# Attention stage of a fused layer: one column-tiled group of value and denominator products late in each unit, in place of several

## The reference

```python
dots = jnp.einsum('bhid,bhjd->bhij', q, k) * d ** (-0.5)
dots = jnp.where(mask[None, None], mask_value, dots)
attn = jax.nn.softmax(dots, axis=-1)
out = jnp.einsum('bhij,bhjd->bhid', attn, v)
...
shared = jax.nn.silu(xf @ sh_gate_w) * (xf @ sh_up_w) @ sh_down_w
```

## Time and profile before

| | us |
|---|---|
| time, median of 3 runs | 5415.98 (5410.62 to 5418.36) |
| the profiled execution: its span | 5418.5 |
| time before stage B's first shared-expert matmuls | about 720 |
| stage B, to its last denominator matmul | about 720 to 2447 |
| PE busy in the span | 5303.0 (98%) |
| DVE busy | 3828.9 (71%) |
| ACT busy | 2615.1 (48%) |
| POOL busy | 3028.9 (56%) |

### The profile page before, as it was taken

How to read it: one execution, slowest core, us unless ns; L and a number is a source line. 1 busy time by engine, 2 the same in 40 slices (tenths; PEclk the granted TensorE clock), 3 DMA queues, 4 the chain that set the end, 5 groups by cost and what they waited for, 6 DMA issues and landing times. The chain is left out here.

```text
span 5418.5 us, 102292 instructions
## 1 busy us (share of the span) xinstructions
PE 5303.0 (98%) x32880; PEld 4440.9 (82%) x32880; DVE 3828.9 (71%) x7311; ACT 2615.1 (48%) x3833; POOL 3028.9 (56%) x2716
## 2 busy tenths in 40 slices
PE   8999989999999999998999999999999999999999
PEld 6888866766666667667999999989999999999786
DVE  6666667778787877775676666766667666666664
ACT  3333333333343333335666666666666666666410
POOL 1222215666666665115777777777777777777514
PEclk9999989999999999998999999999999999999999
DMA  7777764444454444435676677767787676676748
GB/s 239 248 242 255 250 173 129 133 134 119 136 148 135 119 141 118 134 98 119 134 158 112 134 170 150 163 132 167 158 227 158 135 164 129 134 156 113 178 154 289
DMA packets 500414, 864.75 MB, mean 160 GB/s; under 512 B 64388, under 2 KB 165493, under 8 KB 497694
## 3 DMA queue, kind: packets, MB, share of 16 engines
q1 hardware_dynamic: 356014, 567.12, 33.2%
q0 software_dynamic: 140928, 292.13, 29.5%
q10 hardware_dynamic: 3312, 3.47, 0.3%
HBM read 498.49 MB, written 330.47 MB: 153 GB/s over the span
## 5 line engine op out<-in xcount | busy, mean ns | idle before, releaser
L1754 POOL DMA_INDIRECT mid_base<-e_rows,e_ox x556 | 1160.3, 2087 | 372.5 <-POOL e_ox L1749 239.5
L1865 DVE TENSOR_TENSOR e_wgu_lo<-e_wgu,e_wgu_hi 128x2048 fp32r<-128x2048 f32 x278 | 637.5, 2293 | 806.4 <-ACT e_wgu_hi L1788 676.6
L1742 POOL DMA_INDIRECT e_xg<-mid_xn,e_ix x556 | 625.5, 1125 | 336.4 <-POOL e_ix L1739 226.4
L1801 ACT CAST e_xT_hi<-e_ps_t 128x512 fp32r<-128x512 f32 x556 | 299.1, 590 | 929.8 <-PE e_ps_t L1931 929.8
L1069 POOL DMA_INDIRECT mid_ids<-b_pairs,b_cell x512 | 614.3, 1200 | 141.8 <-issue 141.0
L1944 PE MATMUL e_ps_g<-e_xT_hi,e_wgu_hi 128*128 128x256 f32 x2224 | 652.9, 294 | 1.7 <-issue 1.7
L1944 PE MATMUL e_ps_g<-e_xT_lo,e_wgu_hi 128*128 128x256 f32 x2224 | 630.0, 283 | 0.0
L1944 PE MATMUL e_ps_g<-e_xT_hi,e_wgu_lo 128*128 128x256 f32 x2224 | 629.7, 283 | 0.0
L1944 PE MATMUL e_ps_u<-e_xT_hi,e_wgu_hi 128*128 128x256 f32 x2224 | 629.4, 283 | 0.0
L1944 PE MATMUL e_ps_u<-e_xT_lo,e_wgu_hi 128*128 128x256 f32 x2224 | 629.4, 283 | 0.0
L1944 PE MATMUL e_ps_u<-e_xT_hi,e_wgu_lo 128*128 128x256 f32 x2224 | 629.4, 283 | 0.0
(11 more groups left out here) (286 smaller groups left out, 13368.0 us busy)
## 6 DMA issues: line engine op xcount, KB each, us to landing
b_xT_hi<-mid_xT_hi SPq DMA_DIRECT2D x32, 1024.0 KB
b_xT_lo<-mid_xT_lo SPq DMA_DIRECT2D x32, 1024.0 KB
mid_base<-b_x SPq DMA_DIRECT2D x32, 1024.0 KB
e_wgu<-in_gate_w SPq DMA_DIRECT2D x62, 512.0 KB
e_wgu<-in_up_w SPq DMA_DIRECT2D x62, 512.0 KB
e_wd<-in_down_w SPq DMA_DIRECT2D x62, 512.0 KB
ec_cell<-mid_base SPq DMA_DIRECT2D x88, 256.0 KB, 4.9
ab_q<-mid_q_hi SPq DMA_DIRECT2D x82, 256.0 KB, 4.0
```

Of the source, the lines that this page charges most:

```text
L1742: pool.indirect_dma_start(xg[s][:, i, :], None, t["xn"], bass.IndirectOffsetOnAxis(ap=ix[s][:, i:i + 1], axis=0))\
L1754: pool.indirect_dma_start(t[f"base{i}"], bass.IndirectOffsetOnAxis(ap=ox[s][:, i:i + 1], axis=0), rows[s][:, i, :], None, compute_op=ALU.a ...
L1801: act.copy(xT_hi[s][:, i * DC // 2 * RB:(i + 1) * DC // 2 * RB], ps_t[i][:, :]).then_inc(xT_hi_ready, 1)
L1865: dve.tensor_tensor(wgu_lo[s][:, :], wgu[s][:, :], wgu_hi[s][:, :].bitcast(F32), ALU.subtract)\
```

## The change

A table says in which slot each unit's groups stand. Units n = 0, 1 and 2 have all their values and the denominators in one place, in slots 7, 9 and 11. Unit n = 3 has two places: slot 6 with the diagonal and block 0, and slot 12, that is slot 0 of the next unit, with blocks 1 and 2 and the denominators. An item has 5 places where it had 14. The work itself, the other matmuls, and the program order of DVE, ACT, POOL and SP are the same.

```diff
+        TILED = {0: {7: [0]}, 1: {9: [1, 0]}, 2: {11: [2, 0, 1]}, 3: {6: [3, 0], SLOTS: [1, 2]}}
+
         def pv_slots(n, k):
-            if k == 6:
-                return [n]
-            return [kt for kt in range(n) if 7 + 2 * kt == k]
+            return TILED[n].get(k, [])
...
+            def tiled(u, k):
+                n = u % NCH
+                for kt in pv_slots(n, k):
+                    values(u, kt)
+                if k == max(TILED[n]):
+                    denominators(u)
+
...
-                    for kt in pv_slots(n, k):
-                        values(u, kt)
-                    if k == 7 and n == 0:
-                        denominators(u)
-                    if k == 0 and u and (u - 1) % NCH:
-                        denominators(u - 1)
+                    if k == 0 and u:
+                        tiled(u - 1, SLOTS)
+                    tiled(u, k)
...
-            denominators(NU - 1)
+            tiled(NU - 1, SLOTS)
```

## The result

The changed kernel takes 5486.0 us (median of 4 runs, 5479.11 to 5494.25), the kernel before in the same comparison 5417.17 (5410.62 to 5419.56). The ratio is 1.0127, 95% interval 1.0115 to 1.0140: 1.3% slower, some 69 us. The profiled execution's span is 5488.8 us, its time 5490.64.

A forecast was written before the change was run, and what follows sets the result against it. Up to slot 8 of units n = 1 and 2 DVE sets the pace, afterwards PE. 5418.5 + 30 (exposed groups) + 32 (clock falls) = 5480.5 profiled, less 2.5 for the median: 5478 us, range 5430 to 5508.

The forecast's parts named there:

- the forecast case: Whole kernel: exposed groups add 30 us and clock falls 32 us, giving 5478 us; chance 0.49.
- Front set by DVE, tail by PE: Units n = 1 and 2: DVE sets the pace up to slot 8, hiding groups; PE sets it from there on.
- Price of a group: On PE: a lone group costs 1.19 us, a further joined one 0.88; 143 joins at 0.31 save 44 us.
- that rule alone: Rival, PE alone sets the pace: the change only removes drains, all 44 us count, 5372 us; chance 0.11.
- Unit by unit: PE time per unit: n = 0 +1.51, n = 1 +2.65, n = 2 +1.60, n = 3 -3.88; +1.88 us an item, +30 in all.
- The clock: Idle before slot 8, n = 1 and 2: 19 of 32 gaps halve PE's clock, 1.70 us each, 32 us.
- The Trainium skill's warning: Gaps before slot 8: it warns only of longer idle gaps; by it the clock stays, leaving the 30 us alone.
- Waits said to cost nothing: Denominators behind DVE's add, SP's loads and stores, POOL's multiplication and ACT's buffers: added or moved waits cost nothing beside the rest.

The follow-up runs named there:

- The experiment with the later add: Changed kernel with DVE's first add_past of units n = 1 and 2 moved from slot 6 to slot 8: 5382.07 us, ratio 0.9935.
- The run with n = 3 alone: Kernel before with only the units n = 3 as in the changed kernel, n = 0, 1 and 2 as before: 5400.24 us, ratio 0.9962.
- The run with the filler: Changed kernel with two matmuls of constants into ps_d at the end of slot 7 of units n = 1 and 2: 5448.48 us, ratio 1.0058.
- the run with the later reciprocals: Kernel with the first add moved to slot 8, plus two of DVE's four reciprocals of n = 0, 1, 2 moved to slots 9 and 10: 5579.95 us.
- with n = 1 alone: Kernel before with only the units n = 1 as in the changed kernel, n = 0, 2 and 3 as before: 5458.89 us, ratio 1.0077.

## Why the prediction was right

5478 us were forecast, 5486.0 measured, within the range and with the sign; the forecast case came, not a rival. By its steps:

- **Front set by DVE, tail by PE.** Right. PE idles before slot 8 as forecast at about 2.1 us: 2.05 in unit 25. The experiment with the later add shows that in the changed kernel it is the add's place, not DVE's load, that sets slot 8. One thing is missing in it: in the kernel before, PE with its groups was as late as DVE, so the front was not DVE's alone, and moving the add there gave nothing (5420.37).
- **Price of a group.** Right: 0.88 and 0.86 us for further groups in a set. The run with n = 3 alone gave -21 us for 48 joins (15 expected). The Trainium skill (TensorEngine Tiling (Array Packing), section Key Properties) says that a change of tiling mode drains the engine; that run agrees in kind. By that rule alone the whole change would have given 5372; it names a cost, not what hides it.
- **Unit by unit.** The run with the filler has no clock falls, so it shows the terms by themselves: n = 0 +1.61 (forecast +1.51), n = 1 +2.72 (+2.65), n = 2 +1.29 (+1.60), n = 3 -3.70 (-3.88), together +1.92 an item (+1.88). In time it is +32 us against +30.
- **The clock.** Right in kind, mis-sized in both factors: 25 falls, not 19, at 1.5 us each, not 1.70. The product is 37.5 instead of 32. The count came from 3 of 5 gaps of like length elsewhere, which is a small sample; the price took half of each stretch as lost, but the step goes from 0.23 to 0.43 us, less than double, which makes it 1.6. One factor was too low and the other too high, so that the product came this near is in part luck. Some 65 us at half clock were forecast, 25 stretches of 3.4 us make 85.
- **The Trainium skill's warning** (TensorE: Matmul & The Clock Gate, section Why this matters for your kernels) concerns gaps longer than these. The measurement decides: gaps of 1.77 to 2.32 us lowered the clock in 25 of 32 places, and filling them gave 37.5 us back.
- **Waits said to cost nothing.** Right for the denominators, for ACT and POOL, though slot 11's set starts 6.4 us behind slot 8's first matmul at full clock (1455.83 to 1462.23 in the run with the filler), not over 7; the add still ends before it, at 1460.51. SP's queue had slack in this change; in the run with the later reciprocals some 12 us more of delay were more than it had.

The size of the miss, 8 us, is the clock's 5.5 and the units' 2.

What stays open is which gaps lower the clock: in n = 1 a gap of 2.02 us left it at 1.00 and one of 1.92 didn't, and with n = 1 alone 7 of 16 counted instead of 11. Length alone doesn't settle it, and no run here was made to tell more.

## What to carry to other kernels

An engine that is 98% busy need not be the one that sets the pace: find for each stretch which wait ends last, and before moving work out of a stretch ask whether it was hidden there. Work that only fills another engine's delay is free where it stands and costs in full elsewhere, so shorten what it was filling (here, one add placed behind the work that PE waits for) together with moving it: here neither step alone made the kernel faster. Or leave it there, joined: that gained nearly as much. And follow an engine's results through the in-order DMA queue before delaying them: what stands behind a store there is delayed too.

## What the hardware showed that was not expected

- TensorE waits of 1.77 to 2.32 us, between dense matmuls, came in 25 of 32 places with 3.4 us at 1.2 GHz. Two useless full-width matmuls in each of them kept 2.4 GHz and made the kernel 37.5 us faster.
- A fall cost less than half of its stretch, 1.5 of 3.4 us: the step between matmuls of 512 columns went from 0.23 to 0.43 us, less than double.
- Two reciprocals of 0.95 us each, moved five slots later on DVE, cost 198 us by way of one store at the head of SP's queue (5382.07 to 5579.95), and moving one load ahead of that store gave 227 back (5352.85).
